# Mamba layer with a ternary feed-forward on one Trainium2 core: the places of the work in a chunk's 64 units set anew

## The chip, the cores and the metric

The kernel runs on one core of a Trainium2 chip, as one launch. The metric is the device time of that launch in microseconds (us). The engines are TensorE (PE in the profile, its weight loads PEld), VectorE (DVE), ScalarE (ACT), GpSimd (POOL) and SyncE (SP), which only issues DMAs here.

## The reference

The input `x` is 2 sequences of 4096 tokens with 512 features; everything is float32.

```python
xz = einsum('bld,ed->ble', hidden, in_proj_w)          # 512 -> 2048
x, z = xz[..., :1024], xz[..., 1024:]
x = silu(causal_conv4(x) + conv_b)                     # 4 taps over the sequence
x_dbl = einsum('bld,ed->ble', x, x_proj_w)             # 1024 -> 64 + 16 + 16
dt = softplus(x_dbl[..., :64] @ dt_proj_w.T + dt_proj_b)
h_t = exp(dt_t * A) * h_(t-1) + (dt_t * B_t * x_t)     # per channel d (1024) and state n (16)
y_t = sum over n of h_t[d, n] * C_t[n]
y = (y + x * D) * silu(z)
x1 = layernorm(hidden + y @ out_proj_w.T)              # 1024 -> 512
h = relu(x1 @ quantised(W1).T + b1)                    # 512 -> 2048, weights -1, 0, 1
out = layernorm(x1 + h @ quantised(W2).T + b2)         # 2048 -> 512
```

## The kernel before

**Two phases.** The first runs the scan layer over 16 chunks of 512 tokens and stores `x1`; the second quantises the weights and runs the feed-forward over 16 chunks. The change touches the first phase alone (and the bookkeeping of PSUM banks where the first hands over to the second).

**The 64 units of a chunk.** The 1024 channels are 8 blocks of 128 partitions, taken as 4 pairs. With 16 states `n`, a chunk has 4 x 16 = 64 units `u`, and in each the five engines work on one pair and one state:

- SP: `load_bb` (L368) brings row n of B, spread over 128 partitions, into a ring of 4 tiles `bb`, as soon as the product four units back is done.
- POOL: `dbu` (L592) multiplies `dtx` = dt*x of the pair with `bb`. It runs at most one unit ahead of the scans, since `dbu` has two buffers. Before it stands `save_state` (L566), which keeps the last column of h.
- ACT: two `decay` (L639), exp(dt*A), one per block, into two PSUM tiles, for unit u+1. Between them it multiplies the transposed h of unit u-1 with C (`scale_by_c`, L653), two instructions for each half `k`.
- DVE: two scans (L898), h = decay*h + dbu. The first waits, in this order, for the slot of h (three of them), for the saved state, for its decay and last for its product `dbu`; the second for its decay. This function is the same in both kernels.
- PE: transposes h into the PSUM tiles `HT[0]` and `HT[1]` (L1192), four 128x128 blocks for each half, and adds `ch` of unit u-1 into the PSUM tiles `Y` by further transposes (`sum_over_n`, L1197), eight of them.

**Who multiplies by C.** For most units ACT does it and PE adds. For the units in `BY_DVE` (12 of 64) DVE does both: `add_by_c` (L904) reads HT and adds into `ya` in four instructions (L915 the first of a pair, L919 the others); then ACT's four `ch` and PE's eight transposes fall away. HT has one buffer for each half, so PE's transposes of the next unit wait until the half is read.

**The places.** All other work of the layer, for this chunk `c`, the one before `p` and the one after `f`, is put between the units at places written out in tables. ACT and PE have two places in a unit (2u and 2u+1), DVE three (3u before the first scan, 3u+1 between the scans, 3u+2 after the second), POOL and SP one (u, behind the product and, for SP, around `load_bb`).

- PE (`SLOTS`, made by `pe_slots`): in_proj of `z` of this chunk and `x` of the next (L1142), 8 blocks of 4 parts each; out_proj `o` of the chunk before (L1176), 4 blocks of 8 parts; `xd` and `dt` (x_proj, dt_proj), 8 parts each; `ct`, one. A part is two matmul instructions with 512 columns. All of them alternate between two PSUM banks in the order in which they begin (`banks`); `room` waits until the block before in that bank has been read.
- ACT: `TAKE_X` (first tap of the conv out of PSUM), `SILU_X_AT`, `TAKE_XD_AT`, `TAKE_CT_AT`, `TAKE_DT`, `EXP_AT` and `LN_AT` (softplus, in pairs of blocks), `TAKE_Z`, `SILU_Z_AT`, and `NORM_*` (layernorm of the chunk before). A change of function table (ACT_TABLE_LOAD) stands before and behind the Silu and Ln groups.
- DVE: `ADD_AT` (`add_by_c`), `CONV_AT` (taps 1 to 3 of the conv, L855; after the third the bank is free), `ROUND_AT`, `LIFT_AT`, `DT_SUM_AT` (softplus: L872, L878, L884), `SKIP_AT` (L925), `RESIDUAL_AT`, `STATS_AT`, `NORM_SUMS_AT`, `SHIFT_AT`.
- POOL: `EXCESS_AT` (L531), `DTX_AT` (L539), `GATE_AT` (L526), `CORR_AT`, `FIX_AT`.
- SP: the in_proj weights `win` (two slots). Block i is loaded when the block two before it in its slot is through, at a unit that lies 7 units behind the last part of that earlier block: `x` i at unit 22+2i, `z` i at 38, 40, 42, 44, 50, 58 and 60 for i = 1 to 7.

Every engine works its list in order; semaphores tie them together. What isn't ready where it stands holds up all that is behind it on its engine.

Of the kernel before, what the change touches and what calls it, by code (L numbers as in the profile page):

```python
# [69 lines left out]
BY_DVE = (9, 10, 20, 37, 38, 39, 53, 54, 55, 59, 60, 61)  # L70
# [91 lines left out]
def layer(nc, x_tm, x_cm, w_in, conv_w, conv_b, w_xp, w_dt, b_dt, a_log, d_skip, w_out, b_rows, x1, w1, b1, w2, b2, out):  # L162

    ctx = ExitStack()
    with ctx:
# [91 lines left out]
        win_in = {kind: [sem(f"win_{kind}{i}") for i in range(2)] for kind in "xz"}  # L257
# [100 lines left out]
        def _(sp):  # L358
# [64 lines left out]
            load_win("x", 0)  # L423
            load_win("x", 1)
# [11 lines left out]

            def chunk(c, is_first, is_last):
# [5 lines left out]
                for u in range(UNITS):  # L443
                    if u == 0:
                        if is_first:
                            wait_full(sp, "x", c, NB - 1)
                        else:
                            wait_full(sp, "z", p, NB - 1)
                        load_win("z", 0)
                        if not is_last:  # L450
                            load_win("x", 0)
# [6 lines left out]
                    if u == 9 and not is_last:  # L458
                        wait_full(sp, "z", c, 0)
                        load_win("x", 1)  # L460
                    for i in range(2, NB):
                        if u == 22 + 2 * i and not is_last:
                            wait_full(sp, "x", f, i - 2)
                            load_win("x", i)
                    for i, at in ((1, 38), (2, 40), (3, 42), (4, 44), (5, 50), (6, 58), (7, 60)):
                        if u == at:
                            if i >= 3:
# [3 lines left out]
                            elif i == 2:  # L471
                                wait_full(sp, "z", c, 0)
                            load_win("z", i)
                    if u == 49 and not is_last:
# [918 lines left out]
```

## Time and profile before

| | us |
|---|---|
| median of 3 runs | 5187.58 (5177.46 to 5194.58) |
| profiled execution | 5189.64, its span 5187.8, mean granted TensorE clock 0.945 |

Busy time over the whole span, as the first part of the page has it:

```profile
PE 4515.9 (87%) x23362; PEld 3155.1 (61%) x23362; DVE 4051.2 (78%) x4782; ACT 3573.7 (69%) x6726; POOL 3165.4 (61%) x2471
```

The first phase takes about the first 4180 us (POOL has no work in the second). To read a unit's price off such a trace, take the distance from the start of an instruction to the start of the next on that engine, not its duration: neighbours overlap by some tens of ns, and matmuls by more.

### The profile page before, as it was taken

The numbers are of one execution on the slowest core, as the hardware profiler recorded it, in microseconds if no ns is written. First come the engines' busy times: TensorE is split into PE (matmuls) and PEld (weight loads), VectorE is DVE, ScalarE is ACT, GpSimd is POOL, SyncE is SP. The second block draws the span as 40 slices with busy tenths as digits, with TensorE's granted clock in tenths as the row PEclk, the third lists the DMA queues.
The fourth block names the chain that finished last, engine by engine and source line by source line (L and its number), as shares of the span: only waits on it lengthen the run. The fifth ranks groups of instructions, "written<-read, shape, count | busy, mean of one in ns | idle before, by whom it ended". The sixth has DMA issues, their size and how long they took to land.

```text
span 5187.8 us, 85358 instructions
## 1 busy us (share of the span) xinstructions
PE 4515.9 (87%) x23362; PEld 3155.1 (61%) x23362; DVE 4051.2 (78%) x4782; ACT 3573.7 (69%) x6726; POOL 3165.4 (61%) x2471
## 2 busy tenths in 40 slices
PE   5979897989797989897989898888888799999998
PEld 3656565656565656555655555555555568888887
DVE  5888888888888888888888888888888864444454
ACT  5888887878787878787878787878787722222222
POOL 4787868686868686868686868686868600000000
PEclk8999998989999989898989898999998899999999
DMA  3323323332323233333333333232324300110000
GB/s 95 97 89 96 98 93 97 92 100 91 100 90 100 93 99 90 98 90 98 90 98 91 98 91 99 92 102 89 100 90 148 109 17 33 37 43 32 32 32 33
DMA packets 233374, 436.69 MB, mean 84 GB/s; under 512 B 23968, under 2 KB 24096, under 8 KB 232416
## 3 DMA queue, kind: packets, MB, share of 16 engines
q1 hardware_dynamic: 232928, 431.55, 27.0%
q8 instruction: 181, 2.97, 0.2%
q14 instruction: 265, 2.17, 0.1%
HBM read 397.38 MB, written 34.08 MB: 83 GB/s over the span
## 4 chain that ended last, share of the span: by engine, by line
PE 58%; ACT 13%; DVE 13%; issue 10%; POOL 4%; DVEq 1%; ACTq 1%; DMA 0%; POOLq 0%; SPq 0%
PE gemm L1142 13%; PE ht L1192 12%; PE y L1197 9%; PE ht L1319 8%; DVE h L898 7%; PE gemm L1176 5%; ACT ch L653 5%; PE y L1332 4%; PE gemm L1332 4%; ACT decay L639 4%; POOL dbu L592 2%; PE gemm L1152 2%; POOL x L526 1%; ACT dt L683 1%; ACT soft L690 1%
## 5 line engine op out<-in xcount | busy, mean ns | idle before, releaser
L898 DVE TENSOR_TENSOR_SCAN h<-decay,carry,dbu 128x512 f32<-128x512 f32 x2048 | 2522.8, 1269 | 296.0 <-ACT decay L639 178.9
L592 POOL TENSOR_TENSOR dbu<-dtx,bb 128x1024 f32<-128x1024 f32 x1024 | 2458.2, 2401 | 5.6 <-issue 2.4
L639 ACT ACTIVATE decay<-dt,aneg 128x512 f32<-128x512 f32 x2048 | 1429.3, 700 | 689.0 <-DVE h L898 684.7
L1192 PE MATMUL ht<-ident,h 128*128 128x128 f32 x8192 | 1342.5, 292 | 620.5 <-DVE h L898 458.6
L1192 PEld LDWEIGHTS ht<-ident,h 128*128 128x128 f32 x8192 | 1018.6, 149 | 1335.6 <-issue 830.3
L653 ACT ACTIVATE ch<-ht,ct 128x256 f32<-128x256 f32 x3328 | 1401.3, 481 | 110.8 <-PE ht L1192 108.2
L1142 PE MATMUL gemm<-xt,win 128*128 128x512 f32 x2048 | 1063.3, 604 | 11.0 <-DMA win<-w_in 7.2
L1197 PEld LDWEIGHTS y<-ident,ch 128*128 128x128 f32 x6656 | 795.3, 144 | 404.1 <-issue 363.8
L1197 PE MATMUL y<-ident,ch 128*128 128x128 f32 x6656 | 898.5, 279 | 4.2 <-DVE x L925 2.6
L566 POOL TENSOR_TENSOR carry<-h,ones_pair 128x2 f32<-128x2 f32 x1022 | 271.4, 266 | 870.3 <-DVE h L898 860.1
L818 ACT ACTIVATE hr<-ht,b1c 128x512 f32<-128x512 f32 x256 | 176.4, 689 | 707.9 <-PE ht L1319 707.9
L1176 PE MATMUL gemm<-wout,x 128*128 128x512 f32 x1024 | 532.4, 607 | 0.0
L1099 DVE CAST hhi<-hr 128x512 fp32r<-128x512 f32 x256 | 109.4, 427 | 461.6 <-ACT hr L818 461.5
L1319 PE MATMUL ht<-xhi,wq 128*128 128x512 f32 x1024 | 398.9, 390 | 0.8 <-DVE xres L932 0.8
L1319 PE MATMUL ht<-xlo,wq 128*128 128x512 f32 x1024 | 398.8, 389 | 0.0
L1142 PEld LDWEIGHTS gemm<-xt,win 128*128 128x128 f32 x2048 | 317.3, 194 | 28.2 <-issue 20.9
L919 DVE SCALAR_TENSOR_TENSOR ya<-ht,ct,ya 128x256 f32<-128x256 f32 x512 | 221.3, 477 | 116.8 <-PE ht L1192 116.3
L855 DVE SCALAR_TENSOR_TENSOR x<-gemm,cw,x 128x511 f32<-128x511 f32 (+2 forms) x384 | 281.3, 733 | 20.6 <-ACT x L661 15.8
L1319 PEld LDWEIGHTS ht<-xhi,wq 128*128 128x128 f32 x1024 | 192.3, 188 | 42.8 <-DVE xres L932 1.6
L1319 PEld LDWEIGHTS ht<-xlo,wq 128*128 128x128 f32 x1024 | 192.2, 188 | 40.4
L1332 PE MATMUL y<-wq,hhi 128*128 128x512 f32 x512 | 204.7, 400 | 4.0 <-DVE hlo L1101 3.8
L1332 PE MATMUL gemm<-wq,hhi 128*128 128x512 f32 x512 | 200.5, 392 | 0.0
(91 smaller groups left out, 3974.8 us busy)
## 6 DMA issues: line engine op xcount, KB each, us to landing
bb<-b_rows SPq DMA_DIRECT2D x1024, 256.0 KB, 3.3
win<-w_in SPq DMA_DIRECT2D x256, 256.0 KB, 3.7
xt<-x_cm SPq DMA_DIRECT2D x16, 1024.0 KB, 6.8
xres<-x_tm SPq DMA_DIRECT2D x16, 1024.0 KB, 6.9
x<-xres SPq DMA_DIRECT2D x16, 1024.0 KB, 5.1
xr<-x SPq DMA_DIRECT2D x16, 1024.0 KB, 5.4
out<-xr SPq DMA_DIRECT2D x16, 1024.0 KB, 4.3
raw<-w SPq DMA_DIRECT2D x8, 1024.0 KB, 7.5
```

The costliest lines, as they stand in the source:

```text
L566: nc.gpsimd.tensor_tensor(carry[:, c.par, n, pair(q)], h[:, H_SLOT[u], :, TC - 1], ones[:, :], ALU.mult)\
L592: nc.gpsimd.tensor_tensor(dbu[:, u % 2, :, :], dtx[:, pair(q), :], bb[:, u % BB_RING:u % BB_RING + 1, :].to_broadcast([P, 2, TC]), ALU.mul ...
L639: nc.scalar.activation(DA[j][:, :], dt[:, c.par, i, :], ACT.Exp, scale=aneg[:, i, n:n + 1])\
L653: ins = nc.scalar.activation(ch[:, b % 2, tb, :], HT[k][:, tb % 2, :], ACT.Copy, scale=ct[:, c.par, tb, n:n + 1])
L855: nc.vector.scalar_tensor_tensor(x[:, f.par, i, back:], G[BANK["x", i]][:, 0:TC - back], cw[:, i, KC - 1 - back:KC - back], x[:, f.par, i, ...
L898: nc.vector.tensor_tensor_scan(h[:, H_SLOT[u], j, :], DA[j][:, :], dbu[:, u % 2, j, :], carry[:, c.par, n, i:i + 1], ALU.mult, ALU.add).th ...
L1142: ins = nc.tensor.matmul(G[BANK[kind, i]][:, :], win[:, slot, k, :], xt[:, chunk.par, k, :], start=(k == 0), stop=(k == KM - 1))
L1176: ins = nc.tensor.matmul(G[BANK["o", tb]][:, :], x[:, p.par, i, tb * P:(tb + 1) * P], wout[:, i, :], start=(i == 0), stop=(i == NB - 1))
L1192: ins = nc.tensor.transpose(HT[k][:, tb % 2, j * P:(j + 1) * P], h[:, H_SLOT[u], j, tb * P:(tb + 1) * P], ident[:, :])
L1197: return nc.tensor.matmul(Y[j][:, tb * P:(tb + 1) * P], src, ident[:, :], start=begins and tb == 0, stop=False, is_transpose=True, skip_gr ...
L1319: ins = nc.tensor.matmul(HP[j % 2][:, :], w1q[k][:, j * P:(j + 1) * P], part[:, k, :], start=(k == 0 and part is xhi), stop=(k == KM - 1 a ...
L1332: ins = nc.tensor.matmul(OP[tb][:, :], part[:, j % 2, tb * P:(tb + 1) * P], w2q[j // KM][:, j % KM, :], start=(j == 0 and part is hhi), st ...
```

## The change

- `BY_DVE` has 8 units (2, 9, 20, 38, 46, 50, 52, 57) in place of 12.
- Every table of places on PE, ACT, DVE and POOL has new entries. PE's parts are no longer two to a unit in regular rows: a place can hold up to four, or none. A part of the adds on DVE stands up to a whole unit further behind its unit than before.
- The loads of `win` on SP are derived: the 16 blocks of x and z in the order in which PE begins them take the two slots in turn, one semaphore for each slot, and a block is loaded 5 units (`LOAD_LAG`) behind the last part of the block two before it. The load of the next chunk's input `xt` moves from unit 2 to 6 and waits for the last z block of the chunk before; that of `xres` moves from 4 to 5, the store of B from 49 to 55.
- The code that says which block holds which PSUM bank at a chunk's start and end is derived from the same order. `scan` has no edit; its last wait is the one for the product, before and after.

```diff
--- before.py
+++ after.py
@@ -67,7 +67,7 @@
 
 UNITS = (NB // 2) * NS
 NP = NB // 2
-BY_DVE = (9, 10, 20, 37, 38, 39, 53, 54, 55, 59, 60, 61)
+BY_DVE = (2, 9, 20, 38, 46, 50, 52, 57)
 BY_ACT = tuple(u for u in range(UNITS) if u not in BY_DVE)
 HALVES = 2 * UNITS
 H_SLOT = [u % 3 for u in range(UNITS - 4)] + [1, 0, 2, 1]
@@ -86,64 +86,109 @@
 KINDS = {"x": NB, "z": NB, "xd": 1, "ct": 1, "dt": NB, "o": TB}
 
 
+Z_AT = ((0, 4, 8, 9),
+        (67, 70, 71, 72),
+        (73, 74, 75, 75),
+        (77, 79, 82, 87),
+        (101, 102, 103, 104),
+        (105, 105, 105, 106),
+        (107, 108, 108, 108),
+        (109, 111, 112, 113))
+X_GEMM_AT = ((35, 37, 38, 40),
+             (42, 42, 43, 43),
+             (43, 44, 45, 46),
+             (47, 49, 50, 51),
+             (53, 53, 54, 54),
+             (56, 56, 58, 58),
+             (60, 62, 62, 63),
+             (63, 64, 64, 67))
+OUT_AT = ((2, 2, 3, 4, 5, 6, 6, 7),
+          (10, 10, 13, 13, 16, 17, 18, 19),
+          (20, 20, 20, 21, 22, 22, 23, 23),
+          (26, 26, 27, 27, 30, 31, 34, 35))
+XD_AT = (78, 78, 79, 79, 79, 80, 83, 85)
+DT_AT = (92, 93, 93, 94, 96, 98, 99, 101)
+CT_AT = 91
+
+
 def pe_slots():
 
     slots = {}
-    for n in range(KM):
-        slots[n] = [("z", 0, (n,))]
-        for i in range(NB):
-            slots[36 + KM * i + n] = [("x", i, (n,))]
-        for i, at in ((1, (68, 69, 70, 71)), (2, (72, 73, 74, 75)), (3, (76, 77, 86, 87)), (4, (100, 101, 102, 103)),
-                      (5, (104, 105, 106, 107)), (6, (108, 109, 110, 111)), (7, (112, 113, 114, 115))):
-            slots[at[n]] = [("z", i, (n,))]
-    for n in range(NB):
-        for tb in range(TB):
-            slots[4 + NB * tb + n] = [("o", tb, (n,))]
-        slots[78 + n] = [("xd", 0, (n,))]
-        slots[92 + n] = [("dt", n, ())]
-    slots[90] = [("ct", 0, ())]
+    for kind, table in (("o", OUT_AT), ("x", X_GEMM_AT), ("xd", (XD_AT,)), ("ct", ((CT_AT,),)), ("dt", [(at,) for at in DT_AT]),
+                        ("z", Z_AT)):
+        for i, ats in enumerate(table):
+            for n, at in enumerate(ats):
+                slots.setdefault(at, []).append((kind, i, () if kind in ("ct", "dt") else (n,)))
     return slots
 
 
 SLOTS = pe_slots()
-TAKE_X = {41 + 4 * i: i for i in range(NB)}
-SILU_X_AT = 75
-TAKE_Z = {7: 0, 73: 1, 77: 2, 89: 3, 105: 4, 109: 5, 113: 6, 117: 7}
-TAKE_XD_AT, TAKE_CT_AT = 87, 93
-TAKE_DT = {95 + 2 * i: (2 * i, 2 * i + 1) for i in range(NB // 2)}
-EXP_AT = {97: 0, 101: 1, 7: 2, 11: 3}
-LN_AT = {107: (0, 1), 19: (2, 3)}
-SILU_Z_AT = 119
-NORM_LN_AT = 107
-NORM_AT = {113: (0,), 115: (1, 2), 117: (3,)}
-
-ADD_AT = {31: 9, 33: 10, 64: 20, 115: 37, 117: 38, 121: 39, 163: 53, 165: 54, 169: 55, 181: 59, 183: 60, 187: 61}
-CONV_AT = {65 + 6 * i: ((i, 1),) for i in range(NB)} | {67 + 6 * i: ((i, 2), (i, 3)) for i in range(NB)}
-ROUND_AT = {152: (0,), 158: (1,), 17: (2,), 23: (3,)}
-LIFT_AT = {152: (0,), 158: (1,), 17: (2,), 23: (3,)}
-DT_SUM_AT = {170: 0, 173: 1, 38: 2, 41: 3}
-SKIP_AT = {8: ((3, 0), (3, 1))} | {3 * (NS * (q + 1) + 2) + 2: ((q, 0), (q, 1)) for q in range(NP - 1)}
-RESIDUAL_AT = {3 * (7 + 4 * tb) + 2: tb for tb in range(TB)}
-STATS_AT = {117: (0, 1, 2, 3)}
-NORM_SUMS_AT, SHIFT_AT = 117, 164
-
-EXCESS_AT = {56: 0, 57: 1, 12: 2, 13: 3}
-DTX_AT = {60: (0,), 61: (1,), 4: (2,), 6: (3,), 18: (4,), 20: (5,), 22: (6,), 24: (7,)}
-GATE_AT = {61: (0, 1), 62: (2, 3), 63: (4, 5), 3: (6, 7)}
-CORR_AT, FIX_AT = 2, 38
-
-
-def banks():
+TAKE_X = {43: 0, 44: 1, 48: 2, 54: 3, 58: 4, 60: 5, 64: 6, 68: 7}
+SILU_X_AT = 79
+TAKE_Z = {10: 0, 73: 1, 77: 2, 91: 3, 106: 4, 107: 5, 112: 6, 115: 7}
+TAKE_XD_AT, TAKE_CT_AT = 91, 93
+TAKE_DT = {94: (0, 1), 95: (2,), 98: (3,), 99: (4,), 101: (5,), 102: (6,), 104: (7,)}
+EXP_AT = {3: 2, 5: 3, 98: 0, 102: 1}
+LN_AT = {20: (2, 3), 105: (0, 1)}
+SILU_Z_AT = 117
+NORM_LN_AT = 105
+NORM_AT = {109: (0,), 112: (1,), 113: (2,), 118: (3,)}
+
+ADD_AT = {11: 2, 32: 9, 65: 20, 120: 38, 143: 46, 156: 50, 162: 52, 180: 57}
+CONV_AT = {65: ((0, 1), (0, 2)), 67: ((0, 3),), 70: ((1, 1),), 71: ((1, 2),), 73: ((1, 3),), 76: ((2, 1),),
+           81: ((2, 2),), 82: ((2, 3),), 85: ((3, 1),), 86: ((3, 2),), 88: ((3, 3),), 91: ((4, 1),),
+           94: ((4, 2), (4, 3)), 96: ((5, 1),), 97: ((5, 2),), 98: ((5, 3),), 101: ((6, 1), (6, 2)), 103: ((6, 3),),
+           108: ((7, 1),), 109: ((7, 2),), 110: ((7, 3),)}
+ROUND_AT = {15: (2,), 17: (3,), 151: (0,), 158: (1,)}
+LIFT_AT = {10: (2,), 27: (3,), 157: (0,), 159: (1,)}
+DT_SUM_AT = {43: 2, 50: 3, 165: 0, 169: 1}
+SKIP_AT = {5: ((3, 0),), 8: ((3, 1),), 55: ((0, 0),), 56: ((0, 1),), 103: ((1, 0),), 104: ((1, 1),), 149: ((2, 0),),
+           150: ((2, 1),)}
+RESIDUAL_AT = {27: 0, 41: 1, 45: 2, 64: 3}
+STATS_AT = {93: (0,), 98: (1,), 99: (2,), 126: (3,)}
+NORM_SUMS_AT, SHIFT_AT = 158, 163
+
+EXCESS_AT = {12: 2, 14: 3, 54: 0, 55: 1}
+DTX_AT = {2: (2,), 12: (3,), 24: (4,), 30: (5,), 31: (6,), 36: (7,), 56: (0,), 58: (1,)}
+GATE_AT = {2: (6,), 3: (7,), 60: (0, 1, 2), 61: (3,), 62: (4,), 63: (5,)}
+CORR_AT, FIX_AT = 23, 39
+
+XT_AT, X_AT, B_AT = 6, 5, 55
+LOAD_LAG = 5
+
+
+def begun(kinds):
 
     order = []
     for at in sorted(SLOTS):
         for kind, i, _ in SLOTS[at]:
-            if (kind, i) not in order:
+            if kind in kinds and (kind, i) not in order:
                 order.append((kind, i))
-    return {name: n % 2 for n, name in enumerate(order)}
+    return order
+
+
+def banks():
+
+    return {name: n % 2 for n, name in enumerate(begun(KINDS))}
+
+
+def loads(order):
+
+    at = {}
+    for n in range(len(order)):
+        if n < 2:
+            u = 0
+        else:
+            last = max(slot for slot in SLOTS for kind, i, _ in SLOTS[slot] if (kind, i) == order[n - 2])
+            u = min(last // 2 + LOAD_LAG, UNITS - 1)
+        at.setdefault(u, []).append(n)
+    return at
 
 
 BANK = banks()
+WIN_ORDER = begun("xz")
+WIN_LAST = begun("z")
+WIN_AT, WIN_LAST_AT = loads(WIN_ORDER), loads(WIN_LAST)
...
+            def load_win(slot, kind, i):
+                sp.dma_start(win[:, slot, :, :], w_in[i + (NB if kind == "z" else 0)]).then_inc(win_in[slot], 16)
+
+            def load_next_win(c, order, n):
+
+                user = order[n - 2] if n >= 2 else WIN_ORDER[n - 2]
+                owner = c if n >= 2 else c.near(-1)
+                wait_full(sp, user[0], owner.near(1) if user[0] == "x" else owner, user[1])
+                load_win(n % 2, order[n][0], order[n][1])
...
+                    order, at = (WIN_LAST, WIN_LAST_AT) if is_last else (WIN_ORDER, WIN_AT)
+                    for n in at.get(u, ()):
+                        if is_first and n < 2:
+                            wait_full(sp, "x", c, NB - 2 + n)
+                            load_win(n, order[n][0], order[n][1])
+                        else:
+                            load_next_win(c, order, n)
...
-                    if u == 2 and not is_last:
+                    if u == XT_AT and not is_last:
+                        wait_full(sp, "z", p, NB - 1)
                         load_xt(f, tok_f)
-                    if u == 4 and not is_first:
+                    if u == X_AT and not is_first:
                         load_x(p, tok_p)
...
-            def in_proj(kind, chunk, i, parts, room):
-                slot = (i + 1) % 2 if kind == "x" else i % 2
+            def in_proj(kind, chunk, i, parts, room, n, earlier=NB // 2):
+                slot = n % 2
                 if 0 in parts:
                     room(kind, chunk, i)
                     if i == 0:
                         wait(pe, xt_in, chunk, 16, 16)
-                    wait(pe, win_in[kind][i % 2], chunk, NB // 2 * 16, (i // 2 + 1) * 16)
+                    wait(pe, win_in[slot], chunk if kind == "z" else chunk.near(-1), NB * 16, (earlier + n // 2 + 1) * 16)
...
```

## Rows read from the trace of the kernel before

**Rows 1.** Windows of eight units, one steady chunk: busy us (instructions), clock, DMA share, GB/s.

```profile
core 0: us, PE busy (x) PEld busy (x) DVE busy (x) ACT busy (x) POOL busy (x), PEclk, DMA share, GB/s
1858.47:1892.92 34.45, 30.42 (x165) 21.62 (x166) 25.92 (x24) 26.36 (x53) 28.57 (x26) 0.91 0.36 108
1892.92:1923.58 30.66, 26.88 (x132) 16.64 (x131) 27.93 (x30) 22.43 (x42) 26.05 (x19) 0.94 0.21 62
1923.58:1954.16 30.58, 28.38 (x162) 19.15 (x161) 25.80 (x30) 21.52 (x45) 23.70 (x19) 1.00 0.27 79
1954.16:1981.60 27.44, 27.44 (x161) 19.26 (x160) 27.30 (x33) 24.55 (x53) 21.18 (x19) 1.00 0.41 116
1981.60:2017.14 35.54, 29.50 (x170) 19.93 (x167) 32.34 (x47) 29.44 (x54) 20.11 (x16) 0.97 0.34 104
2017.14:2042.76 25.62, 24.21 (x130) 15.99 (x130) 21.52 (x22) 20.27 (x44) 20.36 (x18) 0.91 0.29 84
2042.76:2080.36 37.60, 32.60 (x172) 19.95 (x170) 29.85 (x31) 34.63 (x64) 23.68 (x16) 0.99 0.27 78
2080.36:2116.86 36.50, 23.35 (x103) 15.57 (x104) 28.55 (x35) 26.57 (x44) 33.89 (x26) 0.69 0.36 123
sum 258.39, PE 222.78 PEld 148.11 DVE 219.21 ACT 205.78 POOL 197.55; mean PE 27.85 PEld 18.51 DVE 27.40 ACT 25.72 POOL 24.69
```

**Rows 2.** Chain that ended last, in order of time: start us, us, what.

```profile
1961.24 0.88 PE y L1197 x8
1962.11 0.44 PE ht L1192 x4
1962.55 0.86 PE gemm L1142 x2
```

**Rows 3.** Waits of DVE in 14 steady chunks: us in total, times, longest us.

```profile
DVE h L898 <- ACT decay L639: 161.6, 161, 3.7
DVE ya L919 <- PE ht L1192: 106.0, 159, 1.7
DVE ya L915 <- PE ht L1192: 94.8, 112, 2.8
DVE h L898 <- POOL dbu L592: 61.2, 104, 2.4
```

**Rows 4.** Timeline of ACT: start us, us, instruction.

```profile
2000.62 0.69 ACT L639 ACTIVATE decay<-dt,aneg 128x512 f32<-128x512 f32 x1 [1.23 <-DVE h L898]
2001.25 0.82 ACT L653 ACTIVATE ch<-ht,ct 128x256 f32<-128x256 f32 x2
2001.96 0.60 ACT L704 ACTIVATE z<-gemm 128x512 f32<-128x512 f32 x1
...
2005.26 1.28 ACT L667 ACT_TABLE_LOAD   x1
...
2006.56 3.90 ACT L667 ACTIVATE x<-x 128x1024 f32<-128x1024 f32 x4
```

**Rows 5.** Timeline of DVE.

```profile
1858.47 4.81 DVE L898 TENSOR_TENSOR_SCAN h<-decay,carry,dbu 128x512 f32<-128x512 f32 x4 [1.72 <-PE ht L1192]
...
2076.43 1.65 DVE L919 SCALAR_TENSOR_TENSOR ya<-ht,ct,ya 128x256 f32<-128x256 f32 x4
```

**Rows 6.** Groups of the whole trace on POOL: count | busy us, mean ns | idle before.

```profile
L592 POOL TENSOR_TENSOR dbu<-dtx,bb 128x1024 f32<-128x1024 f32 x1024 | 2458.2, 2401 | 5.6 <-issue 2.4
...
L526 POOL TENSOR_TENSOR x<-x,z 128x512 f32<-128x512 f32 x128 | 159.8, 1270 | 48.8 <-DVE x L925 30.0 <-ACT z L709 18.7
```

**Rows 7.** Line 872, 14 chunks: duration ns min/median/max, first and last start.

```profile
L872 DVE TENSOR_SCALAR rounded<-soft x56: 667/1216/2253, 345.6 to 3864.5; 128x1024 f32<-128x1024 f32 x56
```

**Rows 8.** Timeline of POOL and DVE around one softplus sum.

```profile
1911.31 2.35 POOL L531 TENSOR_TENSOR soft<-soft,rounded 128x1024 f32<-128x1024 f32 x1
1911.60 3.14 DVE L884 SCALAR_TENSOR_TENSOR dt<-soft,dt 128x1024 f32<-128x1024 f32 x1
...
1917.03 1.19 DVE L884 SCALAR_TENSOR_TENSOR dt<-soft,dt 128x1024 f32<-128x1024 f32 x1
```

**Rows 9.** DMA issues: out<-in, count, KB each, median us from issue to landing.

```profile
bb<-b_rows SPq DMA_DIRECT2D x1024, 256.0 KB, 3.3
```

More of the change, by code:

```diff
@@ L256, in layer @@
         alog_in = sem("alog_in")
-        win_in = {kind: [sem(f"win_{kind}{i}") for i in range(2)] for kind in "xz"}
+        win_in = [sem(f"win_in{i}") for i in range(2)]
         xt_in = sem("xt_in")
@@ L361, in load_xt @@
                     .then_inc(xt_in, 16)
-            def load_win(kind, i):
-                block_of = i + (NB if kind == "z" else 0)
-                slot = (i + 1) % 2 if kind == "x" else i % 2
-                sp.dma_start(win[:, slot, :, :], w_in[block_of]).then_inc(win_in[kind][i % 2], 16)
+            def load_win(slot, kind, i):
[5 more added lines that the diff above has]
+                load_win(n % 2, order[n][0], order[n][1])
             def load_bb(c, u):
@@ L422, in _ @@
             load_xt(first, 0)
-            load_win("x", 0)
-            load_win("x", 1)
+            load_win(0, "x", 0)
+            load_win(1, "x", 1)
             sp.dma_start(cw[:, :, :], conv_w).then_inc(weights_in, 16)
@@ L433, in _ @@
                 wait_full(sp, "x", first, i - 2)
-                load_win("x", i)
+                load_win(i % 2, "x", i)
             store_b(first)
@@ L443, in chunk @@
                 for u in range(UNITS):
-                    if u == 0:
[L445 to L451, printed above, removed]
+                    order, at = (WIN_LAST, WIN_LAST_AT) if is_last else (WIN_ORDER, WIN_AT)
[5 more added lines that the diff above has]
+                            load_next_win(c, order, n)
+                    if u == 0:
                         wait(sp, b_out, c, 16, 16)
                     load_bb(c, u)
-                    if u == 2 and not is_last:
+                    if u == XT_AT and not is_last:
+                        wait_full(sp, "z", p, NB - 1)
                         load_xt(f, tok_f)
-                    if u == 4 and not is_first:
+                    if u == X_AT and not is_first:
                         load_x(p, tok_p)
[L458 to L467, printed above, removed]
-                                wait_full(sp, "z", c, i - 2)
-                            elif not is_last:
-                                wait_full(sp, "x", f, NB - 3 + i)
[L471 to L474, printed above, removed]
+                    if u == B_AT and not is_last:
                         store_b(f)
@@ L1132, in _ @@
             pe.wait_ge(ident_set, 1)
-            def in_proj(kind, chunk, i, parts, room):
-                slot = (i + 1) % 2 if kind == "x" else i % 2
+            def in_proj(kind, chunk, i, parts, room, n, earlier=NB // 2):
+                slot = n % 2
                 if 0 in parts:
@@ L1228, in rooms, with held_after, held_at_end @@
                 return room
-            def last_z(p):
+            def held_after(p):
+                order = begun(KINDS)
                 held = [None, None]
-                for i in (NB - 2, NB - 1):
-                    held[BANK["z", i]] = ("z", p, i)
+                for kind, i in order[-2:]:
+                    held[BANK[kind, i]] = (kind, p if kind in "zo" else p.near(1), i)
+                return held
+            def held_at_end(last):
+                held = [None, None]
+                for kind, i in begun("zo"):
+                    held[BANK[kind, i]] = (kind, last if kind == "z" else last.near(-1), i)
                 return held
@@ L1239, in _ @@
             for i in range(NB):
-                in_proj("x", first, i, range(KM), room)
+                in_proj("x", first, i, range(KM), room, i, NB)
             pe.wait_ge(weights_in, 16 * N_WEIGHTS)
@@ L1248, in chunk @@
                 p, f = c.near(-1), c.near(1)
-                room = prologue if is_first else rooms(last_z(p))
+                room = prologue if is_first else rooms(held_after(p))
                 def slot(at):
@@ L1253, in slot @@
                         if kind == "z":
-                            in_proj("z", c, i, parts, room)
+                            n = (WIN_LAST if is_last else WIN_ORDER).index((kind, i))
+                            in_proj("z", c, i, parts, room, n)
                         elif kind == "o":
@@ L1259, in slot @@
                             if kind == "x":
-                                in_proj("x", f, i, parts, room)
+                                in_proj("x", f, i, parts, room, WIN_ORDER.index((kind, i)))
                             elif kind == "xd":
@@ L1289, in _ @@
             sum_over_n(last, UNITS - 1)
-            room = rooms(last_z(last))
+            room = rooms(held_at_end(last))
             room("o", last, 1)
@@ L1297, in _ @@
             transpose_rows(0, 0, 0, range(2))
-            room = rooms(last_z(last))
+            room = rooms(held_at_end(last))
             for tb in range(TB):
```

## The prediction

> **What bounds the kernel now.** I read the page's busy shares and slices first (no engine is full in the first phase, all five fall and rise together), then one steady chunk in eight windows of eight units, then the chain of waits in time, then DVE's waits. The windows [rows 1] show the thing to see: in 258.4 us DVE works 219.2, ACT 205.8, POOL 197.6, PE 222.8, and the engine that is nearly full changes from window to window. Units 24 to 31 run at PE's pace (27.44 of 27.44), the first of units 56 to 63 at POOL's (33.89 of 36.50), units 48 to 55 at ACT's (34.63 of 37.60). So the chunk is a row of local limits, held together by short buffers: decay and product one unit ahead, one HT for each half. What counts is how the work lies, and the sum on each engine only second.
>
> PE's busy time includes overlaps, so I price it from the chain, start to start [rows 2]: eight y transposes 0.87, four h transposes 0.44, one GEMM part 0.86. A unit with two parts and an ACT product is 2 x 0.44 + 0.87 + 2 x 0.86 = 3.47 us, and that is the pace of units 24 to 31 (27.44 / 8 = 3.43). Beside it a bare unit costs DVE two scans, 2.40 (4.81 for four [rows 5]), POOL 2.56 (a product of 2.40 at most [rows 6] and the short copy of h's last column), and ACT 2 x (0.62 + 0.72) = 2.68 (start of decay to start of ch 0.63, ch to the next 0.71 [rows 4]).
>
> **The change part by part.**
>
> *Four units go from DVE to ACT.* DVE loses 4 x 1.6 us of `ya` work a chunk = 6.4 (1.65 for the four of a unit [rows 5]). ACT gains 4 x 2 x 0.72 = 5.8 and PE 4 x 0.87 = 3.5 [rows 4, 2]. My sums over a chunk, start to start, go from DVE 211.5, ACT 202.2, POOL 195.0, PE 202.2 to 205.1, 207.9, 195.0, 205.7. The four engines are then level, all of them 50 us below the chunk's length; nothing in the sums alone forbids or gives a gain.
>
> *The waits of the adds.* DVE stood 106.0 + 94.8 = 200.8 us in 14 chunks for HT before an add [rows 3], over 14 x 12 adds: 1.20 us each, 14.3 a chunk. The cause: an add stood right behind the scan of the next unit, while PE had just begun the transposes. Eight adds at the same price wait 9.6, so 4.8 go. The new places stand later (add 38 at 120, two units behind; 50 at 156, 57 at 180), which shortens DVE's wait but makes PE's next transposes wait for the read. Bounds: nothing of 4.8 is won (PE or ACT holds DVE instead) and all 14.3.
>
> *The places.* I laid both tables over the units with these prices: tap 0.66, skip 0.66, round 0.62, lift 1.13, dt sum 1.12, residual 0.59, stats 0.62 on DVE; first tap 0.66, dt 0.62, z 0.5, exp group 1.95, ln group 1.95 and silu 3.85 (four with 3.90 us [rows 4]) with 2 x 1.28 of table loads each [rows 4] on ACT; gate and dtx 1.27 [rows 6], excess 2.36 on POOL; 0.86 a part on PE. In every eight units the largest of the four sums is a floor:
>
> before 28.6 PE, 26.0 PE, 27.8 PE, 27.8 PE, 32.0 DVE, 24.3 PE, 32.1 ACT, 35.4 POOL: 234.0;
> after 27.8 PE, 28.6 PE, 27.1 DVE, 27.8 PE, 29.5 PE, 23.1 ACT, 32.2 ACT, 30.7 POOL: 226.8.
>
> Against [rows 1] the floor of before lies 24.4 under the chunk's 258.4, of which some 14 are the add waits and the rest imbalance inside the eight. What moves the floors: POOL at units 60 to 63 and 0 to 3 (two gates in each of 61 to 63, two dtx at 60 and 61) is spread to one gate a unit behind the Silu group, -4.7; in units 32 to 39 three adds, four stats and the aggregate no longer stand behind the Silu group of x, -2.5; the two exp groups with two dt copies each are pulled apart. PE's first 38 units don't change: 76 parts before and after, 131.9 us, so the stretch of [rows 2] gets nothing. Finer windows give more (mean over the starts): three units wide 253.0 to 242.8, two wide 264.0 to 249.9. Coarse -7.2, fine -10 to -14. I take -7.2, as the width that certainly can't be bridged by the buffers, and put -1.8 beside it for the adds (somewhat over a third of 4.8, since the sums of PE and ACT grew), together **-9.0 us a chunk**.
>
> *ACT's bursts against what stands beside them.* Moved steps must still find their input. I went through the tight ones. Silu of x at ACT place 79 stands beside x_proj at PE places 78 and 79, which wait for it 2.3 to 5.1 us; behind it are the transposes of unit 39, whose only reader, ACT, is in the same group, so this costs nothing as long as PE has caught up when ACT's 6.4 us end. Ln at 105 waits for round 158 and lift 159 on DVE, 2.2 us behind ACT's decay, while its table load and first half take 2.2: level. x blocks 4, 5, 6 on PE (53, 56, 60) wait for the third tap of the block two before (82, 88, 94), up to 2.2 us, which the two units of lead take. Each is hidden by less than a microsecond: cost 0 to 1 each, in the range.
>
> *The loads.* A `win` block is asked for 5 units behind its predecessor's last part in place of 7, and SP works in order: if PE isn't through, the next `bb` is late. `bb` lands 3.3 us after its issue [rows 9], one unit is 3.5 to 4, and the ring holds four, so SP can stand about a unit. Cost 0, at worst about 1 us for each of 16 loads a chunk. xt (unit 2 to 6, needed at 17) and xres (4 to 5, needed at 9) keep their slack: nothing. B's store (49 to 55) is nearer: DVE's second rounding, after the scans of unit 52, waits for it, and SP reaches 55 when the product of unit 51 is done, two scans, an add, a lift and two scans earlier, 7.5 us. At a few us for a store (the `bb` load's 3.3 is the nearest row) it is just hidden; if it took 10 us it would cost 2.5 a chunk.
>
> *The port of DVE and POOL.* The same rounding step takes 667 ns at the least, 1216 in the median and 2253 at most [rows 7]; a dt sum that began 0.29 us behind a POOL operation of 2.35 us took 3.14 in place of 1.19 and ended with it plus its own time [rows 8]. Twelve such DVE steps a chunk (four rounds, lifts and sums) can meet a POOL operation, for 0 to 2.36 us each; before, the four rounds lost 0.55 each by the median, and the sum of [rows 8] 1.95, so some 4 in all. Their places are new, so this lies between -4 and 12 x 2.36 - 4 = +24; I take 0, the same luck as before. (The Trainium skill, SBUF — State Buffer, "SBUF: two separate sides", has it as an exclusive lock on a port pair: a DVE instruction in a two-port mode or with two SBUF inputs and a GpSimd one that reads SBUF never run together, the later waits for all of the earlier. The trace agrees, with 3.14 against 1.19. By that rule a random place costs half of 2.36 x POOL's share of 0.76, or 0.9 for each of twelve, 11 a chunk, which would turn the sum to +-0; it is the third rival.)
>
> **Sum.** The first and the last chunk lack parts of the work, so 15 chunks: 15 x 9.0 = 135. The second phase isn't touched. Against the profiled execution, 5189.6 - 135 = 5054.6; the median of the runs is 2 us lower, so I say **5055 us**.
>
> **The rivals.**
>
> 1. *ACT and PE give it back.* The 5.8 us that ACT gains come wholly on the path, because from unit 38 on ACT's sum rises from 83.6 to 95.7 while DVE's falls from 87.5 to 79.2. For it: ACT has the most waited-for row, 161.6 us [rows 3]. Against: before, ACT idled 29 of that stretch's 112. Then -9.0 + 5.8 = -3.2 a chunk, -48: 5142.
> 2. *No change.* The new tables balance sums that the chain doesn't follow, waits only move. PE's stretch of units 1 to 37 speaks for it. 5190, within 0.3% (15 us, about what such a measurement can tell).
> 3. *Slower by the port.* Twelve steps meet running POOL operations more than before. From 9.0 / 12 = 0.75 us more for each step the gain is gone; at 1.1 each it is +4.2 a chunk, 5253. For it: the steps are now single and spread (lift 10, 27, 157, 159; round 15, 17, 151, 158) next to a POOL that is busy 76%. Against: the sums at 43, 50, 165, 169 stand like before, near a scan that POOL waits for too.
> 4. *Slower by SP.* At 1 us for each of 16 loads +16 - 9 = +7 a chunk, 5295; it decides from 0.56 us each. For it: lag 5 for 7. Against: before, all of DVE's waits for the product come to 61.2 in 14 chunks [rows 3], so there is slack to eat.
> 5. *More than forecast.* The fine windows hold (-10.2) and the adds' 4.8 come whole: -15 a chunk, 4965.
>
> **How the numbers follow.** Forecast 0.50 (its own range 5000 to 5110), rival 1 0.20, more than forecast 0.10, no change 0.06, port 0.09, SP 0.05. Range: from 4975, which leaves half of the best case out, to 5195, which takes in rival 1 and no change and leaves the slower two out. Faster 0.50 + 0.20 + 0.10 = 0.80, same 0.06, slower 0.14.
>
> **What the changed profile should show.** Chunks of 249 us in place of 258. DVE's waits for HT under 0.6 us for each of eight adds, DVE busy about 212 a chunk. Units 56 to 63 in some 31 to 33 us in place of 36.5; units 24 to 31 still at 27.4, PE full. ACT's share up to 211. Rounding with a median near 1.2, dt sums mostly at 1.2. Wrong if the wait DVE h <- POOL dbu grows over 9 us a chunk (port or SP), or if DVE h <- ACT decay takes up what the adds give.

## The result and the profile after

The changed kernel runs in 4893.98 us (median of 4, 4890.98 to 4895.49) against 5190.06: ratio 0.9434, interval 0.9418 to 0.9449, 296 us less. I had forecast 5055 with a range down to 4975: the direction was right, the size less than half.

The page's busy line of the changed kernel; its span is 4892.7, the mean clock 0.968 (0.945 before):

```profile
PE 4505.8 (92%) x23874; PEld 3201.2 (65%) x23874; DVE 3891.6 (80%) x4526; ACT 3665.1 (75%) x6982; POOL 3158.1 (65%) x2471
```

The same chunk as in [rows 1], again in windows of eight units, with the same columns:

```profile
core 0: us, PE busy (x) PEld busy (x) DVE busy (x) ACT busy (x) POOL busy (x), PEclk, DMA share, GB/s
1732.68:1762.69 30.01, 26.80 (x144) 18.05 (x143) 24.50 (x26) 23.41 (x46) 24.47 (x20) 0.94 0.44 150
1762.69:1791.53 28.84, 28.81 (x159) 19.48 (x158) 25.46 (x26) 25.52 (x50) 27.61 (x19) 1.00 0.24 74
1791.53:1819.10 27.57, 27.56 (x164) 19.36 (x163) 27.20 (x31) 22.84 (x49) 23.16 (x22) 1.00 0.31 97
1819.10:1846.11 27.01, 26.46 (x156) 18.57 (x154) 26.97 (x33) 24.60 (x53) 23.30 (x21) 1.00 0.37 113
1846.11:1875.71 29.60, 29.50 (x173) 20.34 (x171) 28.87 (x36) 25.49 (x52) 23.14 (x19) 1.00 0.33 103
1875.71:1903.02 27.31, 25.95 (x147) 16.85 (x146) 21.77 (x22) 26.46 (x54) 19.61 (x17) 1.00 0.35 107
1903.02:1939.27 36.25, 31.50 (x149) 18.95 (x148) 32.98 (x37) 33.07 (x58) 24.71 (x18) 0.95 0.22 67
1939.27:1970.79 31.52, 22.56 (x142) 18.29 (x140) 22.72 (x22) 30.67 (x58) 30.61 (x26) 0.84 0.40 117
sum 238.11, PE 219.15 PEld 149.89 DVE 210.47 ACT 212.06 POOL 196.63; mean PE 27.39 PEld 18.74 DVE 26.31 ACT 26.51 POOL 24.58
```

The chunk has lost 20.3 us; the mean over 14 steady chunks is 19.9. Set beside the floors of the prediction (27.8, 28.6, 27.1, 27.8, 29.5, 23.1, 32.2, 30.7), five of the eight windows now end within 0.8 of the floor, one of them (units 24 to 31) below it, so these sums are estimates and no hard limit. Units 0 to 7 lie 2.2 over it, 40 to 47 and 48 to 55 some 4 each. Before, all but one lay 1 to 6 above. So the floors fell by 7.2, and what stood above them by 13: 24.4 to 11.3. DVE was busy 8.7 us less and idle 11.5 us less.

DVE's waits in 14 steady chunks, to set against [rows 3] (us in total, times, longest):

```profile
DVE h L933 <- ACT decay L674: 194.6, 138, 3.9
DVE x L960 <- PE y L1232: 67.3, 28, 6.1
DVE h L933 <- POOL dbu L627: 63.8, 105, 1.3
DVE ya L950 <- PE ht L1227: 11.8, 20, 0.9
```

The waits of the adds are nearly gone: 200.8 before, 11.8 now, or 0.1 for each of 112 adds. The wait for the product is what it was (61.2), that for the decay has grown by 2.4 a chunk, that for `y` at a chunk's start from 21.6 to 67.3, 3.3 a chunk. PE has gained too: in 3274 us of the first phase it stood 340.9 us for DVE's scans before its transposes of h, and 32.5 now; in exchange it stands 58.8 for the adds (L954), for which it had no wait of its own before.

The rounding step of [rows 7], same columns:

```profile
L907 DVE TENSOR_SCALAR rounded<-soft x58: 656/666/673, 337.4 to 3651.7; 128x1024 f32<-128x1024 f32 x58
```

### The profile page after: what moved, and what is told of

It is laid out like the page before. It is cut to its first block, busy times and chain, and to the rows that moved or that the text cites. A ratio compares the mean times of both kernels' runs of the same rounds, so it can differ in the third digit from the quotient of the medians.

```text
span 4892.7 us, 86290 instructions
## 1 busy us (share of the span) xinstructions
PE 4505.8 (92%) x23874; PEld 3201.2 (65%) x23874; DVE 3891.6 (80%) x4526; ACT 3665.1 (75%) x6982; POOL 3158.1 (65%) x2471
## 3 DMA queue, kind: packets, MB, share of 16 engines
q1 hardware_dynamic: 232928, 431.55, 28.6%
## 4 chain that ended last, share of the span: by engine, by line
PE 37%; POOL 22%; issue 16%; ACT 14%; DVE 9%; POOLq 1%; DMA 1%; DVEq 1%; ACTq 0%; SPq 0%
POOL dbu L627 17%; PE ht L1363 8%; PE gemm L1177 7%; ACT ch L688 5%; PE ht L1227 5%; PE y L1376 5%; DVE h L933 5%; PE gemm L1376 5%; ACT decay L674 4%; PE y L1232 4%; PE gemm L1202 2%; POOL x L561 1%; POOL carry L601 1%; PE gemm L1187 1%; POOL soft L566 1%
## 5 line engine op out<-in xcount | busy, mean ns | idle before, releaser
L688 ACT ACTIVATE ch<-ht,ct 128x256 f32<-128x256 f32 x3584 | 1516.0, 484 | 85.0 <-PE ht L1227 81.1
L1227 PE MATMUL ht<-ident,h 128*128 128x128 f32 x8192 | 1273.9, 285 | 327.8 <-ACT ch L688 194.7
L1227 PEld LDWEIGHTS ht<-ident,h 128*128 128x128 f32 x8192 | 971.2, 145 | 843.9 <-ACT ch L688 440.1
L1177 PE MATMUL gemm<-xt,win 128*128 128x512 f32 x2048 | 1026.7, 605 | 15.8 <-DMA win<-w_in 7.4
L1232 PEld LDWEIGHTS y<-ident,ch 128*128 128x128 f32 x7168 | 853.5, 144 | 274.5 <-issue 265.3
L1232 PE MATMUL y<-ident,ch 128*128 128x128 f32 x7168 | 963.9, 279 | 2.9 <-DVE x L960 2.5
L1211 PE MATMUL gemm<-wout,x 128*128 128x512 f32 x1024 | 496.4, 595 | 0.0
L1177 PEld LDWEIGHTS gemm<-xt,win 128*128 128x128 f32 x2048 | 339.9, 194 | 197.0 <-issue 183.7
L1211 PEld LDWEIGHTS gemm<-wout,x 128*128 128x128 f32 x1024 | 169.6, 192 | 87.3 <-issue 87.1
```

What stands on the lines that cost most here:

```text
L688: ins = nc.scalar.activation(ch[:, b % 2, tb, :], HT[k][:, tb % 2, :], ACT.Copy, scale=ct[:, c.par, tb, n:n + 1])
L1177: ins = nc.tensor.matmul(G[BANK[kind, i]][:, :], win[:, slot, k, :], xt[:, chunk.par, k, :], start=(k == 0), stop=(k == KM - 1))
L1211: ins = nc.tensor.matmul(G[BANK["o", tb]][:, :], x[:, p.par, i, tb * P:(tb + 1) * P], wout[:, i, :], start=(i == 0), stop=(i == NB - 1))
L1227: ins = nc.tensor.transpose(HT[k][:, tb % 2, j * P:(j + 1) * P], h[:, H_SLOT[u], j, tb * P:(tb + 1) * P], ident[:, :])
L1232: return nc.tensor.matmul(Y[j][:, tb * P:(tb + 1) * P], src, ident[:, :], start=begins and tb == 0, stop=False, is_transpose=True, skip_gr ...
```

## The experiments

Each ran beside the kernel before, on the same chip; 5190 (5186 to 5187 in these sessions) and 4894 are the two ends. The period below is the distance between the first scans of chunk 1 and chunk 15, over 14: 256.4 before, 236.5 after. The theories stood in pairs: the adds' waits (W) or levelling (L), separate shares (S) or the fit of all places (F), the number of adds (N) or their places (P), and at the end local misfits (K) or the whole chunk's fit (C).

**The adds.**

```diff
 b_adds (before)     BY_DVE and ADD_AT as in the changed kernel
 b_late (before)    -ADD_AT = {31: 9, 33: 10, 64: 20, 115: 37, 117: 38, 121: 39, 163: 53, ...
                    +ADD_AT = {32: 9, 35: 10, 65: 20, 116: 37, 119: 38, 122: 39, 164: 53, ...
 a_adds (changed)    BY_DVE and ADD_AT as before
 a_early (changed)  -ADD_AT = {11: 2, 32: 9, 65: 20, 120: 38, 143: 46, 156: 50, 162: 52, 180: 57}
                    +ADD_AT = {10: 2, 31: 9, 64: 20, 118: 38, 142: 46, 154: 50, 160: 52, 175: 57}
```

b_adds: 

> The kernel before with the new eight units for VectorE and their new places, all other tables old. Theory W (the adds' waits and what they hold up are most of the gain): the 14.3 us a chunk of waits and the 6.4 of ya work go nearly whole, -15 a chunk or more, 4970 or below. Theory L (levelling by all tables together; the adds are one share among several): -4 to -8 a chunk, 5070 to 5130.

Measured 5088.71, ratio 0.9815 (0.9796 to 0.9835): -6.0 a chunk, theory L.

b_late: 

> The kernel before with its twelve units, each add one to three places later (32, 35, 65, 116, 119, 122, 164, 167, 170, 182, 185, 188). Theory W: the wait of 1.20 us before each add shrinks to under 0.4 and the time with it, -8 to -10 a chunk, 5040 to 5070. Theory L: the wait only changes its place, PE's next transposes come later by as much; within 1%, 5140 to 5200.

Measured 5135.36, 0.9905 (0.9885 to 0.9924): -3.5 a chunk, just under L's range, far from W's. The wait did shrink and turned up elsewhere, as DVE's waits in 3274 us of the first phase show:

```profile
DVE h L898 <- ACT decay L639: 281.3, 196, 5.2
...
DVE ya L915 <- PE ht L1192: 16.2, 28, 0.7
```

The adds' wait is 16.2 in place of 181.7 in the same stretch of the kernel before, the decay's 281.3 in place of 145.5. And PE now stands 268.3 us for the adds that read HT, where it stood 340.9 for the scans.

a_adds: 

> The changed kernel with the twelve units of before and their old places. Theory W: most of the gain is lost, 5100 or more. Theory L: a third to a half is lost, 4960 to 5040, and the units 0 to 8 and 21 to 37, where few adds stand, keep theirs.

Measured 5319.05, 1.0263 (1.0242 to 1.0284): slower than the kernel before. Both theories are too small; W's "5100 or more" holds, but W had lost in the old kernel.

a_early: 

> The changed kernel with its eight units, but each add as early as in the kernel before (right behind the first or second scan of the next unit: 10, 31, 64, 118, 142, 154, 160, 175). Theory W: 8 x 1.2 us of waits come back, +9 a chunk, about 5030. Theory L: a third of that, +3 a chunk, about 4940.

Measured 5116.81, 0.9868 (0.9848 to 0.9888): +223, or 1.9 us for each add that is moved by one to five places. The five places are those of unit 57's add, from 180 to 175. In the changed kernel this add stands nine places behind the first place of its unit, while every add of the kernel before stands three or four behind; that is further than the "whole unit" (three places) of the section on the change. DVE's own waits for HT make up under half of the 223.

So the same places bring 98 us in the old surroundings and cost 425 when they are taken out of the new ones. The next runs ask whether the other tables behave alike.

**The other tables, one at a time.** a_pe, a_pool and a_dve are the changed kernel with the tables of one engine as before (for DVE all but the adds); b_pool and b_act are the kernel before with POOL's or ACT's tables new; a_lag7 has `LOAD_LAG = 7`.

a_pe: 

> The changed kernel with PE's parts at the regular old places (two to a unit; bank order and loads follow from them). Theory F (each eight units can come down to the floor of their fullest engine only when every engine's places fit together, so undoing any one table loses more than its own share): +5 a chunk or more, 4970 or above, with the loss in units 0 to 23. Theory S (each table brings its own share, PE's sums over eight units are nearly the same before and after): under +1.5 a chunk, 4894 to 4917.

a_pool: 

> The changed kernel with POOL's old places (gates two to a unit at 61 to 63, dtx 0 and 1 at 60 and 61, and so on). Theory F: over +5 a chunk, 4970 or above, and not in units 56 to 3 alone. Theory S: the floor of units 56 to 63 goes from 30.7 back to 35.4, +4 a chunk there and nothing elsewhere, 4940 to 4960.

a_dve: 

> The changed kernel with VectorE's old places for all but the adds (conv, softplus, skip, residual, stats, aggregate). Theory F: +5 a chunk or more, 4970 or above; the four stats and the aggregate behind the Silu group alone cost 3. Theory S: +1 to +3, 4910 to 4940.

b_pool: 

> The kernel before with POOL's new places alone. Theory S (a table brings its own share): its floors go from 234.0 to 229.7, -4 a chunk, 5120 to 5135, and the gain of one table in the old kernel is about what taking it out of the new one loses (180). Theory F (the gain is in the fit of all): under 1.5 a chunk either way, 5165 to 5210.

b_act: 

> The kernel before with ScalarE's new places alone. Floors 234.0 to 234.1, so theory S: 5180 to 5195. Theory F: a lone table set for other neighbours misses its inputs and loses, 5200 or more.

a_lag7: 

> The changed kernel with LOAD_LAG 7 as before in place of 5. Both theories: if the shorter lag brought something (a win block there in time), this loses 0.5 to 2 a chunk, 4900 to 4925; if SP stood at its waits with lag 5 (my fourth rival), this gains, 4870 to 4890; else within 0.2%.

| | us | ratio to before (interval) | against 4894 / 5187 |
|---|---|---|---|
| a_pe | 5170.04 | 0.9977 (0.9965 to 0.9989) | +276 |
| a_pool | 5074.06 | 0.9793 (0.9772 to 0.9814) | +180 |
| a_dve | 5067.57 | 0.9781 (0.9760 to 0.9803) | +174 |
| b_pool | 5367.54 | 1.0358 (1.0334 to 1.0382) | +181 |
| b_act | 5561.83 | 1.0724 (1.0700 to 1.0747) | +375 |
| a_lag7 | 4896.40 | 0.9452 (0.9431 to 0.9473) | +2 |

S falls in all five, and is wrong even in sign for one: b_pool should have gained 4 a chunk. F holds for a_pe, a_pool, a_dve and b_act. For b_pool F was wrong as well, since it expected no change, and for a_pe it looked for the loss in units 0 to 23, while 12.1 of 18.5 us lie in 38 to 53. A table that is needed in the new kernel can be a loss in the old one. The losses of taking one out add up to 425 + 276 + 180 + 174 = 1055, against 296 gained by all; ACT's table was not taken out of the changed kernel, so its loss there isn't known. A floor says nothing of this: for b_pool it falls by 4.3, and the kernel gets slower by 11 a chunk, while DVE waits 215.6 us for its product in 3274 us (61.2 in 3590 before [rows 3]). The loads' lag is worth nothing either way.

The waits of the two POOL runs show entries that miss their neighbours. In a_pool the old places of `excess` (units 56 and 57) stand behind the new places of the dt sums that need it (165 and 169, in units 55 and 56): DVE stands 113.6 us for POOL there, in 26 waits of up to 5.0 us, and units 54 to 56 lose 5.7 of the 11.6 us a chunk. In b_pool the new place of `dtx` 0 (unit 56) stands ahead of the old place of its dt sum (170, at the end of unit 56): POOL stands 77.8 us for DVE, 6.5 in each of 12 chunks, and what is behind it on POOL is the product.

**Number or place.**

```diff
 a_12late (changed)
-BY_DVE = (2, 9, 20, 38, 46, 50, 52, 57)
+BY_DVE = (2, 6, 9, 20, 38, 43, 46, 50, 52, 54, 57, 61)
+ADD_AT: 23: 6, 134: 43, 167: 54, 188: 61 besides
```

> The changed kernel with twelve units for VectorE again: its eight at their places and 6, 43, 54, 61 added, each as late as the new ones (23, 134, 167, 188). Theory N (the number of adds cost what the twelve of before lose, 425 us): +10 a chunk or more, 5050 or above. Theory P (their places do, the number moves 6.4 us of DVE work against 5.8 of ACT and 3.5 of PE): within 3 a chunk, 4850 to 4940.

Measured 4961.90, 0.9570 (0.9550 to 0.9590): +68, 1.1 us for each unit and chunk. That lies between the two theories' ranges, close to P. If four adds more cost 68 us wherever they stand, the other 357 of the 425 us of a_adds belong to the places; that the two simply add up is assumed, no run shows it.

**A wait that looks like a gain.**

```diff
 a_skip (changed)
-SKIP_AT = {5: ((3, 0),), 8: ((3, 1),), ...
+SKIP_AT = {7: ((3, 0),), 8: ((3, 1),), ...
```

> The changed kernel with the skip of the chunk before's block 6 at place 7 in place of 5, two scans later. DVE stands 4.5 us for it in unit 1 of each chunk. Theory F: what it waits for (PE, which stands idle 3.2 us at a chunk's first units) holds the whole chain, so the wait turns up at the next scans: within 0.3%, 4880 to 4910. Theory S: the wait goes, -2 to -4 a chunk, 4835 to 4865.

Measured 4893.31, 0.9441 (0.9420 to 0.9462), no different from the changed kernel. Units 1 and 2 took 5.7 and 3.9 us in the mean; now they take 2.7 and 7.0. The wait went one unit on, as F said. PE stands still there (the last section has more on it); its timeline in the changed kernel at that point:

```profile
1732.80 1.04 PE L1232 MATMUL y<-ident,ch 128*128 128x128 f32 x8
1737.04 1.11 PE L1227 MATMUL ht<-ident,h 128*128 128x128 f32 x4 [3.21 <-ACT ch L688]
```

**Local or whole.** The unit lengths of two runs (from one unit's first scan to the next one's) repeat to a few hundredths wherever the neighbours are the same: in units 4 to 37 the mean lengths of the three runs below differ from the changed kernel's by 0.03 us at most. If that is the rule, single misfits can be forecast in us.

```diff
 a_pe_mid (changed)   z3 at (76, 77, 86, 87), xd at 78 to 85, ct at 90, dt at 92 to 99, z4 at 100 to 103
 a_one38 (changed)    -120: 38   +118: 38
 a_trio (changed)     unit 57 at 180 -> units 59, 60, 61 at 181, 183, 187
```

a_pe_mid: 

> The changed kernel with PE's old places only in units 38 to 51: z3 (76, 77, 86, 87), xd (78 to 85), ct (90), dt (92 to 99), z4 (100 to 103). Theory K (a misfit is local: the same neighbours give the same unit length whatever the rest of the chunk does): a_pe lost 12.1 of its 18.5 us a chunk in units 38 to 53, so this loses 12.1 x 15 = 182, 5060 to 5090. Theory C (the fit of the whole chunk decides, losses don't split by place): under 60 or over 250.

a_one38: 

> The changed kernel with one add, that of unit 38, at 118 in place of 120 (behind the first scan of unit 39 and not behind its second). Theory K: a_early lost 3.0 us a chunk in units 38 to 41, so +45, 4930 to 4950. Theory C: within 15 of 4894, since seven adds of eight fit and 2.5 us of the Silu group's 6.4 stood idle there anyway.

a_trio: 

> The changed kernel with 59, 60, 61 at 181, 183, 187 as before in place of unit 57 at 180: three adds in a row, each behind the scan that follows its unit, of which the first two hold up PE's transposes of the next. Theory K: a_adds lost 6.1 us a chunk in units 57 to 63, so +92, 4970 to 5000, of which the two added units are worth some 2 a chunk (a_12late: 4.3 for four). Theory C: under 40 or over 150.

Measured 5082.30 (0.9796, 0.9773 to 0.9820), 4949.95 (0.9548, 0.9524 to 0.9571) and 4995.22 (0.9632, 0.9608 to 0.9656): +188, +56, +101 where K said +182, +45, +92. Theory K. The two findings go together: entries that stand within a unit or so of each other, on whatever engine, must fit (F), and the losses of misfits further apart add up (K). Adding up is shown for these three places alone.

What such a misfit is can be read off one place. The changed kernel at unit 39, ACT and DVE:

```profile
1873.22 1.36 ACT L674 ACTIVATE decay<-dt,aneg 128x512 f32<-128x512 f32 x2
1873.99 1.66 DVE L950 TENSOR_SCALAR ya<-ht,ct 128x256 f32<-128x256 f32 x4 [0.54 <-PE ht L1227]
1874.60 1.28 ACT L702 ACT_TABLE_LOAD   x1
1875.57 2.45 DVE L933 TENSOR_TENSOR_SCAN h<-decay,carry,dbu 128x512 f32<-128x512 f32 x2
...
1881.92 2.52 DVE L933 TENSOR_TENSOR_SCAN h<-decay,carry,dbu 128x512 f32<-128x512 f32 x2 [3.90 <-ACT decay L674]
```

And a_one38, where the add stands one scan earlier:

```profile
1900.24 1.66 DVE L950 TENSOR_SCALAR ya<-ht,ct 128x256 f32<-128x256 f32 x4 [1.78 <-PE ht L1227]
1901.81 3.62 DVE L933 TENSOR_TENSOR_SCAN h<-decay,carry,dbu 128x512 f32<-128x512 f32 x3
1903.12 0.69 ACT L674 ACTIVATE decay<-dt,aneg 128x512 f32<-128x512 f32 x1 [2.91 <-DVE h L933]
1903.83 1.28 ACT L702 ACT_TABLE_LOAD   x1
...
1911.16 2.53 DVE L933 TENSOR_TENSOR_SCAN h<-decay,carry,dbu 128x512 f32<-128x512 f32 x2 [5.72 <-ACT decay L674]
```

In both the Silu group of 6.4 us (four activations with a table load before and behind them) stands in ACT's list behind the second decay of unit 40, and that decay waits for the second scan of unit 39. In the first, this scan goes before the add: the decay is out at once, and the add is done while ACT is in its group. In the second the scan stands behind the add and its wait for PE, so ACT idles 2.91 ahead of its longest group, and DVE pays at the other end, 5.72 in place of 3.90. From unit 38's first scan to the table load it is 6.35 us in the one (from 1868.25) and 9.34 in the other (from 1894.49). One add moved by one scan costs 3.0 us in units 38 to 41 and 3.6 over the whole chunk.

The largest misfit of a_pe_mid, 5.7 of its 13.6 us a chunk, in unit 51:

```profile
2015.49 0.69 ACT L718 ACTIVATE dt<-gemm,bdt 128x512 f32<-128x512 f32 x1
...
2016.23 2.07 PE L1202 MATMUL gemm<-rounded,wdt 64*128 64x512 f32 x2 [3.45 <-ACT dt L718]
...
2021.09 0.88 DVE L950 TENSOR_SCALAR ya<-ht,ct 128x256 f32<-128x256 f32 x2 [4.62 <-PE ht L1227]
...
2025.47 0.69 ACT L674 ACTIVATE decay<-dt,aneg 128x512 f32<-128x512 f32 x1 [5.50 <-DVE h L933]
```

PE's dt part stands too early for its bank: it waits 3.45 for ACT's copy. Behind it are the transposes that DVE's add needs, behind the add the scan, behind the scan ACT's decay. Three engines stand one after the other for one GEMM part of 0.86 us. A part of the loss is PE's clock: over the 6 us from 2016 on the granted clock is 0.52, 0.50 and 0.50, where it was 1.00 before the stall. PE takes 4.61 us from the start of this dt part to the GEMM part behind the transposes (2016.23 to 2020.84), and by the prices of [rows 2] it would be 0.86 + 0.87 + 0.44 = 2.17: an estimate of 2.4 of the 5.7 us.

## Why the prediction was wrong in size

- *The failed step* is the sum's last one: "I take -7.2 ... and put -1.8 beside it for the adds". The floors' -7.2 is what the tables level out, and five of eight windows came out near the floors I had for them. But of the 24.4 us above the floors I let only 1.8 go. It was the larger part: -13.1. The runs show how much single entries weigh: in the kernel before, new places and a new number for the adds alone took off 6.0 a chunk (b_adds) and later places alone 3.5 (b_late); in the changed kernel old places of PE, one add a scan earlier and the old trio of adds cost 13.6, 3.6 and 6.3 a chunk (a_pe_mid, a_one38, a_trio, by the mean unit lengths). Whether the same entries cost as much in the kernel before, with its other tables, isn't shown.
- *The stretch I gave nothing.* "PE's first 38 units don't change" holds for PE's work, 76 parts before and after, but I let it stand for the time: by my floors units 0 to 31 even grew by 1.1. Units 0 to 37 are 9.3 us shorter in the mean of 14 chunks, nearly half of the 19.9. In the first three windows PE stood idle 10.0 us before (95.7 less 85.7) and 3.3 now.
- *The waits of the adds* were sized as 1.20 each and four of them gone. In the changed kernel nearly all are: 0.8 a chunk are left of 14.3. My reason against it, that a later add makes PE's transposes wait instead, is what happened in the old surroundings (b_late: 13 less waiting, only 3.5 gained, PE waiting 268.3 us for the adds). In the changed kernel it is true in part, with 58.8 us in the same 3274, 4.2 a chunk.
- *Fewer adds*: forecast 6.4 less for DVE, 5.8 more for ACT; measured 8.7 less (with the port's share) and 6.3 more. Four adds more, at late places, cost the changed kernel 68 us (a_12late); what fewer adds bring in the kernel before was not measured apart from their places.
- *Rival 1, ACT gives it back*: no. DVE's wait for the decay went up by 2.4 a chunk, inside a gain of 20.
- *Rival 3, the port*: the other way round. The four roundings now take 666 ns each in every chunk, where 1216 was the median; over all DVE lines of that kind (round, lift, dt sum, shift) the whole trace has 270 us in place of 299, -1.8 a chunk, and -2.5 without the shift, for the twelve steps that I had counted. I had 0 with bounds of -4 to +24. It is not tested by a run of its own, only read off both traces.
- *Rival 4, SP*: a_lag7 shows no cost and no gain of the lag.
- *Rival 5* named both things that happened (the fine windows and the whole of the adds) and stopped at 4965 with a chance of one in ten. The two-unit windows gave -14.1, with the adds' 4.8 -18.9: near the 19.9 of the period. But that is no reason to trust them. Their sums, 264.0 and 249.9, lie above the chunks themselves, 258.4 and 238.1, so they are no floors: either the prices are too high or the buffers bridge two units in places. One close difference between two such sums can be luck. What is shown is that the coarse sums were too careful, not which width is right.
- *Windows*: units 24 to 31 nearly unchanged (27.44, 27.01), right. Units 56 to 63 -5.0 for -4.7 in this chunk, -3.7 in the mean of 14. The reason given for the -4.7 was not the right one: all six gates stand in units 60 to 63 after the change too (three of them in unit 60), and both dtx stay in the window; what leaves it by the prices are the two `excess` of 2.36 us, from 56 and 57 to 54 and 55. Units 32 to 39 -5.9 for -2.5. Units 0 to 23 came out 9.3 shorter for a floor 1 higher: there a_adds loses 7.7 again, a_pool 4.0, a_pe 3.1 and a_dve 1.2, which together is more than was gained.
- *The clock* has no term in the sum; all of PE's prices are those of the full clock. By the clock column and an estimate (time at half clock, 1.2 of 2.4 GHz, is twice what the mean lacks to 1.00) about 40 us of the chunk of [rows 1] passed at half clock, and about 17 now. What this is worth in the 296 no run separates. It doesn't rule the time by itself: a_pe runs at a mean of 0.957 in 5170 us, a_trio at 0.953 in 4995.
- *A slip of 2 us*: 135 off the median of 5187.6 would have been 5052.6, not 5055. It changes nothing.

What stays open: only about half of a_pool's loss is traced to entries (above). That of a_dve is spread; units 38 and 39, where the four stats stand behind the Silu group again, lose 2.1 of its 11.5, and unit 56 loses 2.8. No run prices the port or the clock alone, and none takes ACT's table out of the changed kernel.

## What to carry to other kernels

Where five engines are tied by buffers one unit deep, the sums per engine tell roughly what a schedule can reach and nothing of where it stands; price an entry by what is behind it on its own engine and what waits for that, unit by unit. One place here (unit 39) also suggests this: ahead of a long group on one engine, put what the group waits for on the other engines before their own extra work, and do the extra work beside the group. Such tables are one change: put into the kernel before singly, one gained and two lost, though the whole gained 5.7%.

## What the runs showed of the hardware

- PE stands still for 3.2 to 3.5 us near the start of chunks 3, 5, 7, 9, 11 and 13. The first part of it is a wait for ACT's `ch`, but PE goes on only 1.7 to 2.1 us after that is done (in chunk 7 done at 1735.31, PE's next at 1737.04; in chunk 8 PE follows within 0.05). The loop's body holds two chunks, and these six begin a second or later pass; chunk 1, where the first pass begins, and 15, behind the loop, have no gap over 0.73. So the stall goes with the jump back. Its cause isn't shown; the DMA share is 0.81 in the 8 us from 1736 on, and 0.36 in the 36 us before. Unit 1 takes 6.2 to 9.2 us in these six chunks and 4.4 in the others; before, unit 2 took 8.2 to 10.6 in four of the six and 3.7 to 5.0 in all others. Moving DVE's wait there changes nothing (a_skip).
- The granted clock rose where PE idles less: 0.69 before and 0.84 after in the last eight units, where PE was busy 64% and 72% of the time, and 0.945 to 0.968 in the mean. In a_pe_mid it fell from 1.00 to 0.52 behind a stall of PE of 3.45 us.
